# Delta mixer of a four-layer stack: the triangular inverse is doubled through its transpose alone

## The reference, cut to what matters

```python
def step(S, xs):
    qt, kt, vt, gt, bt = xs
    S = S * jnp.exp(gt)[..., None, None]
    kv = jnp.einsum('bhk,bhkv->bhv', kt, S)
    delta = (vt - kv) * bt[..., None]
    S = S + jnp.einsum('bhk,bhv->bhkv', kt, delta)
    o = jnp.einsum('bhk,bhkv->bhv', qt * scale, S)
    return (S, o)
```

## Time and profile before

| | |
|---|---|
| time, median of 3 runs | 4643.38 us (4642.2 to 4644.19) |
| span of the profiled execution | 4638.9 us |
| its own time | not listed apart from the span; the span is 4.5 us below the median of the runs |
| PE busy | 4098.6 us (88%) |
| DVE busy | 2752.3 us (59%) |
| ACT busy | 1462.1 us (32%) |
| POOL busy | 1126.2 us (24%) |

### The profile page before, as it was taken

The page is one execution under the profiler, slowest core; times in us unless marked ns, Lnnn a source line. Parts: engine busy times, 40 slices in busy tenths (PEclk is TensorE's granted clock), DMA queues, the critical chain, the costliest instruction groups (busy, mean ns, idle before and its releaser), DMA issues. The chain is left out here.

```text
span 4638.9 us, 62483 instructions
## 1 busy us (share of the span) xinstructions
PE 4098.6 (88%) x22102; PEld 3348.7 (72%) x22102; DVE 2752.3 (59%) x6121; ACT 1462.1 (32%) x2529; POOL 1126.2 (24%) x786
## 2 busy tenths in 40 slices
PE   4858799996899999989998998998999998699999
PEld 2323587884787778877877877887887787578787
DVE  5454455543666766666666666666666667445554
ACT  3232323222333333333333333333323333232321
POOL 1111202000332333233233323323422332220200
PEclk9979899997999999999999999999999999899999
DMA  1000212112000000000000000000000000121301
GB/s 70 9 27 9 100 55 82 55 37 85 1 1 1 19 1 1 19 1 1 19 1 1 19 1 1 19 2 1 19 1 1 6 10 10 47 72 45 109 30 43
DMA packets 54095, 119.89 MB, mean 26 GB/s; under 512 B 2849, under 2 KB 4129, under 8 KB 52769
## 3 DMA queue, kind: packets, MB, share of 16 engines
q1 hardware_dynamic: 53792, 116.03, 7.1%
HBM read 90.85 MB, written 25.17 MB: 25 GB/s over the span
## 5 line engine op out<-in xcount | busy, mean ns | idle before, releaser
L1029 POOL TENSOR_TENSOR b_Aj<-b_At,b_joins 128x512 f32<-128x512 f32 x384 | 545.3, 1438 | 590.3 <-DVE b_At L1400 329.2
L1695 PE MATMUL banks<-b_Tt,b_em 128*128 128x64 f32 x3072 | 564.3, 276 | 0.7 <-ACT b_em L1175 0.7
L1615 PE MATMUL banks<-b_x_cur,b_w_cur 128*128 128x256 f32 x2048 | 499.8, 395 | 38.4 <-ACT b_w_cur L1089 37.6
L1330 DVE SCALAR_TENSOR_TENSOR b_conv<-b_raw,b_taps,b_conv 128x256 f32<-128x256 f32 x768 | 477.2, 683 | 46.9 <-ACT b_conv L1126 46.9
L1693 PE MATMUL banks<-b_em,b_Tt 128*128 128x64 f32 x2560 | 498.8, 277 | 0.0
L1615 PEld LDWEIGHTS banks<-b_x_cur,b_w_cur 128*128 128x128 f32 x2048 | 393.5, 198 | 106.8 <-issue 54.8
L1695 PEld LDWEIGHTS banks<-b_Tt,b_em 128*128 128x128 f32 x3072 | 457.7, 194 | 2.4 <-ACT b_em L1175 0.8
L765 PE MATMUL banks<-f_x_hi,f_w_hi 128*128 128x512 f32 x1024 | 408.1, 399 | 39.7 <-ACT f_silu L634 21.7
L765 PE MATMUL banks<-f_x_lo,f_w_hi 128*128 128x512 f32 x1024 | 405.5, 396 | 0.0
L765 PE MATMUL banks<-f_x_hi,f_w_lo 128*128 128x512 f32 x1024 | 405.4, 396 | 0.0
L1693 PEld LDWEIGHTS banks<-b_em,b_Tt 128*128 128x128 f32 x2560 | 396.0, 195 | 0.0
(11 more groups left out here) (247 smaller groups left out, 7316.5 us busy)
## 6 DMA issues: line engine op xcount, KB each, us to landing
f_x_tok<-rows SPq DMA_DIRECT2D x16, 1024.0 KB, 7.5
b_w_load<-in_b_qkvz SPq DMA_DIRECT2D x8, 1536.0 KB, 7.3
f_stage<-in_ffn_gate SPq DMA_DIRECT2D x8, 1024.0 KB, 6.4
f_stage<-in_ffn_up SPq DMA_DIRECT2D x8, 1024.0 KB, 7.5
f_stage<-in_ffn_down SPq DMA_DIRECT2D x8, 1024.0 KB, 4.9
f_x_res<-rows SPq DMA_DIRECT2D x8, 1024.0 KB, 5.6
f_part<-f_x_res SPq DMA_DIRECT2D x8, 1024.0 KB, 4.3
f_x_res<-f_part SPq DMA_DIRECT2D x8, 1024.0 KB, 5.4
```

Source lines behind the costliest of these rows:

```text
L1029: pool.tensor_tensor(f.Aj[:, i % 2, :, :], f.At[:, :, :], joins[:, i:i + 1, :].to_broadcast([P, U, P]), ALU.mult).then_inc(f.s["joined"], 1)
L1330: dve.scalar_tensor_tensor(f.conv[:, i, :, :], raw[:, i, :, tap:tap + P], taps[:, i, tap:tap + 1], f.conv[:, i, :, :], ALU.mult, ALU.add). ...
L1615: mm = pe.matmul(bank[i][:, 2 * a:2 * a + 2, :], w_cur[:, k, col:col + P], f.x_cur[:, k, :, :], start=(k == 0), stop=(k == KD - 1))
L1695: mm = pe.matmul(packed(f.right, i + 1, u), f.X[:, u, :], half_of(f.Tt, u, i + 1, 1), start=True, stop=True)
```

## The change

At each level only the transpose Tt is updated. The product L1693 and the DVE addition L1427 are gone. In their place PE transposes the updated Tt back into the bank `left` at levels 1 to 5 (`turn_back`, four transposes), and ACT copies the half of T that the level needs (`turned_back`). The order of the two flights changes as well: step i is now turn_back(A, i), y(B, i-1), x(A, i), turn_back(B, i), y(A, i), x(B, i), and x(B, 0) comes right behind first_blocks(B). The lists of ACT and DVE follow; POOL's list is as it was.

```diff
-    TN = 1 + 2 * LV
+    TN = 2 + LV
...
+            def turned_back(f, m, i):
+                act.wait_ge(f.s["Tps"], LV * m + i + 1)
+                act.wait_ge(f.s["px"], LV * m + i)
+                act.copy(half(f.T, i + 1, 0), half(f.left, i + 1, 0)).then_inc(f.s["T0"], 1)
...
+                level(B, m, 0)
                 for i in range(1, LV):
+                    turned_back(A, m, i)
                     level(A, m, i)
-                    level(B, m, i - 1)
+                    turned_back(B, m, i)
+                    level(B, m, i)
                 from_state(A, m)
-                level(B, m, LV - 1)
...
             def level(f, m, i):
                 dve.wait_ge(f.s["py"], LV * m + i + 1)
-                dve.wait_ge(f.s["T"], TN * m + 2 + 2 * i)
-                if i == 0:
-                    dve.wait_ge(f.s["T0"], m + 1)
-                if i < LV - 1:
-                    dst = half(f.T, i + 1, 0)
-                    dve.tensor_tensor(dst, dst, packed(f.left, i + 1), ALU.add).then_inc(f.s["T"], 1)
-
+                dve.wait_ge(f.s["T"], TN * m + 2 + i)
...
                 for i in range(1, LV):
+                    level(B, m, i - 1)
                     level(A, m, i)
-                    level(B, m, i - 1)
                     if i < TAPS and not last:
                         convolve(A, 2 * m + 2, i)
...
+            def turn_back(f, m, i):
+                pe.wait_ge(f.s["T"], TN * m + 2 + i)
+                for u in range(U):
+                    mm = pe.transpose(f.left[:, u, :], f.Tt[:, u, :], ident[:, :])
+                mm.then_inc(f.s["Tps"], 1)
+
             def level_x(f, m, i):
                 if i == 0:
-                    pe.wait_ge(f.s["T0"], m + 1)
                     pe.wait_ge(f.s["atm"], 2 * m + 2)
+                pe.wait_ge(f.s["T0"], LV * m + i + 1)
                 pe.wait_ge(f.s["joined"], LV * m + i + 1)
-                pe.wait_ge(f.s["T"], TN * m + (1 + 2 * i if i > 0 else 2))
...
             def level_y(f, m, i):
                 pe.wait_ge(f.s["X"], LV * m + i + 1)
-                pe.wait_ge(f.s["T"], TN * m + 2 + 2 * i)
+                pe.wait_ge(f.s["T"], TN * m + 2 + i)
                 for u in range(U):
-                    if i < LV - 1:
-                        pe.matmul(packed(f.left, i + 1, u), f.Tt[:, u, :], half_of(f.X, u, i + 1, 0),
-                                  start=True, stop=True)
...
                 first_blocks(B, m)
+                level_x(B, m, 0)
                 for i in range(1, LV):
+                    turn_back(A, m, i)
+                    level_y(B, m, i - 1)
                     level_x(A, m, i)
-                    level_x(B, m, i - 1)
+                    turn_back(B, m, i)
                     level_y(A, m, i)
-                    level_y(B, m, i - 1)
+                    level_x(B, m, i)
                 from_state(A, m)
-                level_x(B, m, LV - 1)
```

More of the change, by code:

```diff
@@ L1166, in first_blocks @@
             def first_blocks(f, m):
-                act.wait_ge(f.s["Tps"], m + 1)
+                act.wait_ge(f.s["Tps"], LV * m + 1)
                 act.wait_ge(f.s["o"], m)
                 act.copy(f.T[:, :, :], f.right[:, :, :]).then_inc(f.s["T0"], 1)
+            def turned_back(f, m, i):
+                act.wait_ge(f.s["Tps"], LV * m + i + 1)
+                act.wait_ge(f.s["px"], LV * m + i)
+                act.copy(half(f.T, i + 1, 0), half(f.left, i + 1, 0)).then_inc(f.s["T0"], 1)
             def level(f, m, i):
```

## The result

The changed kernel takes 4781.07 us (median of 4 runs, 4769.07 to 4812.77) against 4643.62 us for the kernel before (4 runs beside it, 4642.2 to 4644.19): a ratio of 1.0313, 95% interval 1.0273 to 1.0352. It is slower, as forecast, but by three times as much, and outside the range. The profiled execution took 4792.09 us, with a span of 4790.3 us, 151.4 us more than that of the earlier trace rows.

A forecast was written before the change was run, and what follows sets the result against it. PE alone was taken to bound the loop. Saved PE work less waits and late DVE summed to +20 us, low clock added 23 us: 4682 us against the profiled 4638.9, 4686 us as median; range 4612 to 4740 us.

The forecast's parts named there:

- x(B, 0): Right behind first_blocks(B), PE waits for the whole-tile copy of T: 0.91 us a pair.
- PE work: Removed L1693 products less ten added turn_backs a pair: net PE work falls by 4.6 us a pair.
- ten waits for X: PE waits 0.27 us between x and y for the X copy, ten times a pair: 2.7 us.
- T copies: ACT's copy of half of T, covered by a y of the other flight: no wait, at most 0.02 us each.
- DVE late, step 2: turn_back(B, 2) waits for DVE, held by step 1's convolutions that POOL instructions meet: 0.5 us a pair.
- DVE late, step 4, without / with `chunk_of_x(A)`: turn_back(B, 4) waits for DVE, held by step 3's convolutions: 0.7 us, or 1.6 where chunk_of_x(A) joins.
- a spell of half that length: Low clock in step 4 of 16 pairs with `ahead`, half the earlier 6.83 us spell: 16 x 1.46 = +23 us.
- Rival 1: Same waits, but the clock stays at 1.00 in the loop: 4663 us; chance 0.22.
- Rival 4: Clock falls in every pair for about two loop steps (10 us): 138 us more, 4800 us; chance 0.12.
- Rival 2: DVE never late, POOL's joins missing the convolutions: a pair gains 1.0 us, 4611 us; chance 0.14.
- Rival 3: Low spell before B's keys is luck; sparing every second pair returns 47 us: 4616 to 4639 us; chance 0.16.
- The stretch of the convolutions: Four convolutions on DVE take 1.67 us with POOL idle, about 1.0 us more for each POOL instruction met.

The follow-up runs named there:

- experiment 3: Kernel before, with y(A, 4) made to wait for four extra ACT copies that lead nowhere; 4931.45 us, ratio 1.0632.
- experiment 1: Changed kernel with POOL's chunk_of_x(A) held back until from_state(A) is done; 4651.44 us, ratio 1.0025.
- experiment 6: Changed kernel with the 256-column projection of q and k moved from behind the loop to right behind y(A, 4); 4653.3 us, ratio 1.0032.
- experiment 2: Changed kernel with four unread products (0.89 us) put ahead of turn_back(B, 4), DVE as late as before; 4660.16 us, ratio 1.005.
- experiment 7: Changed kernel with convolutions split around level(A, i) on DVE: 4608.86 us, ratio 0.9933; with chunk_of_x(A) also held back: 4607.87 us, 0.9936.
- experiment 5: Changed arithmetic in the order of the kernel before, x(A, i) and x(B, i-1) together again, likewise the y; 4640.23 us, ratio 0.9993.
- experiment 10: Four filler products ahead of the last pair's x(B, 0): changed kernel with chunk_of_x(A) held back, 4646.04 us; second, split kernel with projection fills, 4575.39 us.
- experiment 9: Changed kernel with convolutions split, chunk_of_x(A) held back, and PE's remaining waits filled with z and q, k projection work; 4566.05 us, ratio 0.984.

## Why the prediction was wrong

**Right.** What is worth time on PE and where: PE alone bounded the loop. The chain was right in its order, its places and its cause, read from the starts of the records: waits for X in front of y, one of 0.89 us (forecast 0.91) in front of x(B, 0), waits for DVE in front of turn_back(B, 2) and (B, 4), the latter longest where `chunk_of_x(A)` meets the convolutions. That the clock falls there, and the price of a low microsecond: (41.0 - 33.73 - 0.8) / 14.7 = 0.44 us, forecast 0.43; the 0.8 is what the longer wait costs in itself (34.56 - 33.73). In experiment 3, whose loop has hardly any other wait, the price is nearer 0.48: loops 310 us longer, some 47 of them pauses, for 550 us of low clock.

**The terms of the sum at full clock** were near, most of them a little too dear, the T copies too cheap. Read from the starts in the pair at 2515.37 (the last row's second figure in the pair at 2324.26). A late DVE is taken net, less the waits for X and T that vanish behind it. The profile's own idle times hardly show the small waits (4.2 us in all in front of L1698), because records overlap.

| term, us a pair | forecast | measured |
|---|---|---|
| PE work | -4.6 | -4.3 (y(A, 0) gave 0.56 of its 0.89) |
| ten waits for X | 2.7 | 2.0 (0.20 each) |
| x(B, 0) | 0.91 | 0.89 |
| T copies | 0 to 0.02 each | 0.05 each, 0.45 |
| DVE late, step 2 | 0.5 | 0.28 |
| DVE late, step 4, without / with `chunk_of_x(A)` | 0.7 / 1.6 | 0.53 / 1.3 |
| sum | +0.2 / +1.1 | -0.15 / +0.6 |

With these terms alone the change would cost some 13 us (23 x 0.6 less 8 x 0.15), 0.3%; experiment 1, with the shorter wait in every pair but the last pair's spell still in it, measured +0.25%.

**The step that failed** is "I take a spell of half that length, an estimate, in these 16 pairs: 16 x 1.46 = +23 us". Three things in it were wrong. The pairs with `ahead` are 23, not 16: three of the four pairs of each head, less the last one; that was a miscount. The spell is 14.7 us long in the mean and not 3.4. Its length was taken from the earlier trace rows, where the spell lies over the key products and wider ones ahead of the loop; behind the wait in the loop come products of 64 columns, and the clock stayed down through them. Experiment 6, with wide products next to the same wait, has spells of 6.8 us at most. So the term is 22 x 14.7 x 0.44 = 142 us. And the last pair was not seen at all: "first_blocks(B) needs a Tt that DVE has ready before the shorter y(A, 0) and the projection are over" names a projection that this pair lacks; its loop takes 18.9 us more, with 47.8 us of low clock. The account closes: loops 3.4 (8 pairs x 0.43) + 1.3 (the one at full clock) + 169 (22 x 7.7) + 19 = 193 of 194 us; less 18 and 24 outside, 151 us. That the change came out slower, as forecast, is the chain's doing in small part only; nearly all of it is the clock.

**The rivals.** Rival 1, the waits with the clock at 1.00, is near to what experiment 2 makes of pairs 0 to 30: 4660 us against its 4663. Rival 4 had the size (4800), with another place and cause: a fall in every pair, from many small waits and from transposes in place of products. Experiment 1 keeps both and has no fall in 31 pairs; experiment 3 has neither and falls in all 32.

The Trainium skill, "TensorE: Matmul & The Clock Gate", "Part 4: PE-mode transpose", says that transposes do not count as busy in the way products do; the traces here don't bear that out as a cause, since eight pairs of the changed kernel and 31 of experiment 1 keep clock 1.00 with all their transposes in the loop.

Rival 2, DVE never late, is what experiment 7 made true, and with it the gain of about 1 us a pair came: 4609 us against its 4611. Rival 3, luck with the spell before the keys of B, was not what gave time back: from the keys to the first blocks of B the clock is low in 27 pairs instead of 16 (113 us instead of 100), and that stretch is shorter by 19 us, of which y(A, 0) makes 18. The 24 us came mostly from between the keys of A and those of B, where the low clock fell from 108 to 62 us and the time by 15 us; no run here tells why.

**The stretch of the convolutions** was forecast at about 1.0 us for each POOL instruction that meets them. The 3.75 us agree: taken one by one, the four last 0.77 us (met by the end of a join), 1.49 (the last join), 1.25 (`chunk_of_x(A)`) and 0.47. The Trainium skill, "SBUF — State Buffer", "SBUF: two separate sides", says that a DVE instruction with two inputs in SBUF and a GpSimd instruction that reads SBUF lock each other out for a whole instruction; the 0.87 and 2.37 us for two convolutions in experiment 7, without and with a join under way at their start, agree with that.

**Open.** Why the same pause brings the fall in one pair and not in another (the pause of 1.00 us in 9 of 31 pairs in experiment 5, that of 1.38 us in 9 of 23 in experiment 6 and in 22 of 23 in the changed kernel, those of 1.03 and 1.06 us between wide products in none). In the last pair a fall came behind 0.94 us in front of first_blocks(B), while 12 other pairs of the same run (the second of experiment 10) waited 1.03 us there, beside projection products, without one. What ends a spell: in the changed kernel the wide products behind the loop, in experiment 5 some ended among narrow ones.

## What to carry to other kernels

When a change takes work from the engine that bounds a loop and lengthens the chain beside it, look for the longest single wait that comes of it, in the last iteration too, and not at the sum of the waits. Price that wait twice: at its length, and at the low clock that may follow through the whole stretch of narrow products behind it. A wait of a microsecond on TensorE, among narrow products, is worth filling, with work that is due or even with products that nobody reads.

## What the runs showed of the hardware

Pauses of TensorE, as the profile records its idle time, and the clock behind them. Among float32 products of 64 columns: 0.39, 0.48, 0.59 and 0.72 us, no fall behind any of them in pairs 0 to 30; 1.00 us, a fall in 9 of 31 (experiment 5); 1.26 us (experiment 3; 1.18 in four pairs) and 1.38 us (changed kernel), a fall in 54 of 55. With products of 256 columns near on both sides: 1.03 us in 11 pairs (experiment 9) and 1.06 us in 31 (experiment 5), no fall. With wide products behind it alone (experiment 6) the same 1.38 us cost 3.4 to 6.8 us of low clock, or none. In the last pair, where no projection stands near, the fall came behind each pause of 0.91 to 1.66 us in front of first_blocks(B), and not behind 0.41 us in the kernel before.

Once down, the clock stayed there for 13.7 to 17.1 us in most pairs of the changed kernel and of experiment 3 (10.2 and 20.5 us in three), for 3.4 or 13.7 us in experiment 5, and for 44 to 48 us in the last pair in the new order, with PE busy in 47.67 of 47.80 us.

A VectorE instruction with two inputs in SBUF (0.47 us alone) took up to 1.49 us where a GpSimd instruction was under way (2342.05, changed kernel). The update of Tt, with one input in PSUM, kept its 0.48 us beside a join (2268.37, experiment 7).
